# Graph layers and attention on one core: fourth sweep's sums and bias on TensorE with five tile pairs fetched ahead; fifth sweep's residual in one step

## The reference, cut to what matters

```
h = relu(adj @ (x @ W1) + b1)             # layer 1: 20 columns, second sweep
h = relu(adj @ (h @ W2) + b2)             # third sweep
h = relu(adj @ (h @ W3) + b3)             # fourth sweep: adj @ h has 20 columns, W3 makes 128
x = layernorm(x + relu(h + x))
fc = x @ W + b                            # layer 2, fifth sweep
x = layernorm(x + (adj * dinv[:,None] * dinv[None,:]) @ fc)
x = layernorm(x + adj @ x + gamma * attention(x))      # layer 3: sixth sweep, then attention
```

## Time and profile before

| | |
|---|---|
| median of 3 runs | 1342.76 us (1340.31 to 1343.25) |
| the profiled execution | 1341.3 us, span 1339.5 us |
| fourth sweep, from its first epilogue_1 to the end of its tiles | 454.3 to 530.8 us |
| fifth sweep | 530.8 to about 723 us |
| sixth sweep | to about 907 us |
| attention | the rest |
| granted TensorE clock | 0.994 of full, 1.00 in all the stretches below |

### The profile page before, as it was taken

How to read it: one execution, slowest core, us unless ns; L and a number is a source line. 1 busy time by engine, 2 the same in 40 slices (tenths; PEclk the granted TensorE clock), 3 DMA queues, 4 the chain that set the end, 5 groups by cost and what they waited for, 6 DMA issues and landing times.

```text
span 1339.5 us, 17278 instructions
## 1 busy us (share of the span) xinstructions
PE 1285.0 (96%) x5911; PEld 792.2 (59%) x5911; DVE 930.6 (69%) x1207; ACT 715.7 (53%) x880; POOL 267.5 (20%) x175
## 2 busy tenths in 40 slices
PE   8999999999999899999999999998899999999987
PEld 3544444433232233778787788886677767767764
DVE  6666665551010365999999989896888788788885
ACT  1111111011110123688787877776788788788795
POOL 0111110010000010011111100005234334354345
PEclk9999999998999999999999999999999999999999
DMA  9886665555999899899999999970000000000000
GB/s 367 314 316 251 251 219 204 173 188 181 382 333 400 309 352 407 307 353 374 351 371 359 376 356 361 382 291 0 1 0 1 1 1 1 1 18 14 1 1 32
DMA packets 81087, 288.01 MB, mean 215 GB/s; under 512 B 9466, under 2 KB 11130, under 8 KB 81018
## 3 DMA queue, kind: packets, MB, share of 16 engines
q1 hardware_dynamic: 78768, 286.30, 57.2%
q10 hardware_dynamic: 2250, 0.82, 0.2%
HBM read 284.98 MB, written 2.10 MB: 214 GB/s over the span
## 4 chain that ended last, share of the span: by engine, by line
PE 79%; DVE 8%; ACT 4%; issue 4%; DMA 3%; POOL 1%; POOLq 0%; ACTq 0%; DVEq 0%; SPq 0%
PE acc L1298 17%; PE acc L1536 7%; PE acc L1454 7%; PE acc L1388 7%; PE acc L1449 6%; PE acc L1450 6%; DMA raw<-in_adj_s 3%; DVE t_lo L1029 2%; PE rs L1306 2%; PE acc L1526 2%; PE acc L1527 2%; PE acc L1530 2%; PE e L1491 2%; PE e L1493 2%; PE rs L1491 2%
## 5 line engine op out<-in xcount | busy, mean ns | idle before, releaser
L1029 DVE TENSOR_TENSOR t_lo<-raw,t_hi 128x1024 fp32r<-128x1024 f32 x256 | 311.1, 1259 | 26.7 <-ACT t_hi L743 21.8
L743 ACT ACTIVATE t_hi<-raw 128x1024 fp32r<-128x1024 f32 x256 | 261.5, 1054 | 40.5 <-PE acc L1454 39.9
L1449 PE MATMUL acc<-t_hi,st_hi 128*128 128x512 f32 x512 | 201.9, 394 | 0.9 <-ACT t_hi L743 0.9
L1450 PE MATMUL acc<-t_hi,st_lo 128*128 128x512 f32 x512 | 199.5, 390 | 0.0
L613 POOL TENSOR_TENSOR ring_lo<-ring,p_hi 128x1024 fp32r<-128x1024 f32 x64 | 155.4, 2429 | 220.0 <-ACT p_hi L799 219.9
L1298 PE MATMUL acc<-raw,x 128*128 128x512 f32 x400 | 179.3, 597 | 0.0
L1454 PE MATMUL acc<-t_lo,st_hi 128*128 128x512 f32 x512 | 159.5, 393 | 5.8 <-DVE t_lo L1029 5.0
L1103 DVE TENSOR_TENSOR ring<-ring,e 128x1024 f32<-128x1024 f32 x128 | 154.0, 1212 | 0.1
L793 ACT ACTIVATE ring<-ring 128x1024 f32<-128x1024 f32 x128 | 134.2, 1054 | 25.0 <-DVE ring L1103 24.9
L1298 PEld LDWEIGHTS acc<-raw,x 128*128 128x128 f32 x400 | 73.7, 190 | 92.0 <-issue 92.0
L1536 PE MATMUL acc<-ring,x 128*128 128x512 f32 x256 | 120.2, 592 | 0.0
(11 more groups left out here) (220 smaller groups left out, 1878.8 us busy)
## 6 DMA issues: line engine op xcount, KB each, us to landing
raw<-in_adj_s SPq DMA_DIRECT2D x506, 512.0 KB, 5.7
kept_t<-in_adj_s SPq DMA_DIRECT2D x8, 512.0 KB, 6.6
x<-in_x SPq DMA_DIRECT2D x4, 512.0 KB, 10.3
kept_x<-in_adj_s SPq DMA_DIRECT2D x4, 512.0 KB, 6.4
kept_e<-in_adj_s SPq DMA_DIRECT2D x4, 512.0 KB, 7.7
kept_l<-in_adj_s SPq DMA_DIRECT2D x4, 512.0 KB, 6.5
kept_s<-in_adj_s SPq DMA_DIRECT2D x4, 512.0 KB, 6.7
kept_v<-in_adj_s SPq DMA_DIRECT2D x4, 512.0 KB, 6.9
```

Of the source, the lines that this page charges most:

```text
L743: nc.scalar.activation(t_hi[:, g % HL, :], raw[:, k, :], ACT.Copy).then_inc(hi_done, 1)
L1029: nc.vector.tensor_tensor(t_lo[:, k, :], raw[:, slot_no(s, c, g), :], t_hi[:, k, :].bitcast(F32), ALU.subtract).then_inc(lo_done, 1)
L1449: mm(a[:, :], block_of(st_h, b), hi[:, m], start=(g == 0 and j == 0), stop=False)
L1450: mm(a[:, :], block_of(st_l, b), hi[:, m], start=False, stop=False)
```

## The change

In the fourth sweep the copy from PSUM to `at` goes to ScalarE (`evacuate`), without adding `sums`. TensorE's epilogue_1 now adds three products for each of four blocks into e0: a constant 1/128 times the bias, `sums` times w3 (for c = 2 to 7), and `at` times w3. VectorE's bias step is gone. Five blocks (ten tiles) of the rows c = 2, 1 and 0 are no longer streamed through the ring: they are loaded into rooms whose tiles are used up, each as soon as the row named in ROOM_FREE is done.

In the fifth sweep the residual is one operation per block of 128 columns (times dinv, plus xb), four instead of two of 512 columns; residual_2 does nothing there. The remainder st5_lo goes from GpSimd to VectorE, after tile 12 of the rows from c = 2 on, and after tiles 3 and 13 of the sixth sweep's first row. 

```diff
-    "resid": (0, 3, 4), "b3": (3,), "lb": (3,), ...
+    "resid": (0, 3), "lb": (3,), ...
+AHEAD_3 = ((2, 4), (2, 5), (1, 3), (1, 4), (0, 2))
+ROOM_FREE = (0, 1, 2, 3, 3)
 def held(s, c, d):
-    return d in KEPT[c] and not (s == 0 and c == LATE)
+    return d in KEPT[c] and not (s == 0 and c == LATE) or s == 3 and (c, d) in AHEAD_3
...
+            def load_ahead(n):
+                c, d = AHEAD_3[n]
+                wait_row(sp, 3, ROOM_FREE[n])
+                for h in range(2):
+                    sp.dma_start(kept_tile(3, c, d, h), tile(c, 2 * d + h)).then_inc(ahead_in[n], 16)
...
                     sp.dma_start(raw[:, i.seq % RAW, :], tile(c, g)).then_inc(raw_in[i.seq % RAW], 16)
+                    while to_load and i.seq >= RAW and row_of[i.seq - RAW] > (3, ROOM_FREE[to_load[0]]):
+                        load_ahead(to_load.pop(0))
...
             def evacuate(s, c, par):
-                if s in NARROW:
+                if s in (1, 2):
                     return
...
                 elif s == 3:
+                    chunk = row(s, c)
+                    if stored(2, chunk):
+                        pe.wait_ge(sums_done, stored(2, chunk))
                     for b in range(CB):
-                        i = mm(block_of(e0, b), block_of(at, b), w3[:, :], start=True, stop=True)
+                        mm(block_of(e0, b), ones_d[:, 0:1].broadcast_to([P, P]), bias3[:, :], start=True, stop=False)
+                        if stored(2, chunk):
+                            mm(block_of(e0, b), block_of(sums[:, chunk, :], b), w3[:, :], start=False, stop=False)
+                        i = mm(block_of(e0, b), block_of(at, b), w3[:, :], start=False, stop=True)
...
                     elif s == 3:
-                        nc.vector.tensor_tensor(blocks(xs[:, :]), blocks(e0[:, :]), over_blocks(bias3[:, :]),
-                                                ALU.add).then_inc(S["b3"], 1)
-                        dve.wait_ge(S["b3"], done("b3", s, c))
                         dve.wait_ge(S["xb"], done("xb", s, c))
-                        nc.vector.scalar_tensor_tensor(out=xs[:, :], in0=xs[:, :], scalar=0.0, in1=xb[:, :],
+                        nc.vector.scalar_tensor_tensor(out=xs[:, :], in0=e0[:, :], scalar=0.0, in1=xb[:, :],
                                                        op0=ALU.max, op1=ALU.add).then_inc(S["t1"], 1)
                     else:
-                        nc.vector.tensor_tensor(blocks(xs[:, :]), blocks(e0[:, :]), spread(cols(dinv, c, CB)),
-                                                ALU.mult).then_inc(S["t1"], 1)
+                        dve.wait_ge(S["xb"], done("xb", s, c))
+                        scale = cols(dinv, c, CB)
+                        for b in range(CB):
+                            i = nc.vector.scalar_tensor_tensor(
+                                out=block_of(xs, b), in0=block_of(e0, b), scalar=scale[:, b:b + 1],
+                                in1=block_of(xb, b), op0=ALU.mult, op1=ALU.add)
+                        i.then_inc(S["t1"], 1)
...
+                    if s == S4 and g == 12 and not (isinstance(c, int) and c < 2):
+                        stationary5_lo(c - 2)
+                    if s == S5 and first(c) and g in (3, 13):
+                        stationary5_lo(NC - 2 if g == 3 else NC - 1)
```

More of the change, by code:

```diff
@@ L56, with summed @@
 }
+def summed(s):
+    return "t1" if s == 4 else "resid"
 def done(stage, s, r):
@@ L270, in build @@
         late_in = sem("late_in")
+        ahead_in = [sem(f"ahead_in{n}") for n in range(len(AHEAD_3))]
         S = {k: sem(f"s_{k}") for k in STAGES}
@@ L361, in wait_row, with kept_tile @@
                 eng.wait_ge(pe_acc, row_end(s, r))
-        def kept_tile(c, d, h):
+        def kept_tile(s, c, d, h):
+            if s == 3 and (c, d) in AHEAD_3:
+                n = AHEAD_3.index((c, d))
+                region, base = ((kept_v, 0), (kept_s, 0), (kept_l, 0), (kept_t, 0), (kept_t, 2))[n]
+                return region[:, base + h, :]
             n = 2 * KEPT[c].index(d) + h
@@ L370, in tile_of @@
         def tile_of(s, r, i):
-            return kept_tile(row(s, r), i.d, i.h) if i.kept else raw[:, i.seq % RAW, :]
+            return kept_tile(s, row(s, r), i.d, i.h) if i.kept else raw[:, i.seq % RAW, :]
         def wait_tile(eng, s, r, i):
             c = row(s, r)
+            if s == 3 and (c, i.d) in AHEAD_3:
+                eng.wait_ge(ahead_in[AHEAD_3.index((c, i.d))], 32)
+                return
             if not i.kept:
@@ L487, in load_kept @@
                     for h in range(2):
-                        sp.dma_start(kept_tile(c, d, h), tile(c, 2 * d + h)).then_inc(res_in, 16)
+                        sp.dma_start(kept_tile(0, c, d, h), tile(c, 2 * d + h)).then_inc(res_in, 16)
             def load_late():
@@ L493, in load_late @@
                     for h in range(2):
-                        sp.dma_start(kept_tile(LATE, d, h), tile(LATE, 2 * d + h)).then_inc(late_in, 16)
+                        sp.dma_start(kept_tile(0, LATE, d, h), tile(LATE, 2 * d + h)).then_inc(late_in, 16)
+            def load_ahead(n):
[3 more added lines that the diff above has]
+                    sp.dma_start(kept_tile(3, c, d, h), tile(c, 2 * d + h)).then_inc(ahead_in[n], 16)
+            row_of = {i.seq: (s, r) for (s, r), here in ITEMS.items() for i in here if not i.kept}
+            to_load = list(range(len(AHEAD_3)))
             def flat(s, r):
@@ L507, in flat @@
                         if s == 0 and c == 0:
-                            sp.dma_start(kept_tile(c, i.d, i.h), tile(c, g)).then_inc(row0_in[g], 16)
+                            sp.dma_start(kept_tile(s, c, i.d, i.h), tile(c, g)).then_inc(row0_in[g], 16)
                         continue
@@ L567, in step @@
                 ps, pc = before(s, c)
-                if s == S4 and not (isinstance(c, int) and c < 2):
-                    stationary5_lo(c - 2)
-                if s == S5 and first(c):
-                    stationary5_lo(NC - 2)
                 if has_before and ps in STAGES["xb"]:
@@ L583, in step @@
                     nc.gpsimd.tensor_copy(cols(x, row(ps, pc)), xn[:, :]).then_inc(S["xw"], 1)
-                if s == S5 and first(c):
-                    stationary5_lo(NC - 1)
             chunks(pool, step)
@@ L644, in evacuate @@
                     act.wait_ge(pe_acc, c + 1)
+                elif s == 3:
+                    wait_row(act, s, c)
                 else:
@@ L878, in stationary_lo, with stationary5_lo @@
                                         ALU.subtract).then_inc(st_lo_done, 1)
+            def stationary5_lo(d):
+                dve.wait_ge(st5_hi_done, d + 1)
+                nc.vector.tensor_tensor(cols(st5_lo, d), cols(x, d), cols(st5_hi, d).bitcast(F32),
+                                        ALU.subtract).then_inc(st5_lo_done, 1)
             def evacuate_narrow(s, r):
-                if s not in NARROW:
+                if s not in (1, 2):
                     return
```

16 lines of the change are left out of this document (6 added, 10 removed).

## The result

| | before | after |
|---|---|---|
| median | 1341.37 us (1338.35 to 1344.23, 16 runs) | 1344.20 us (1341.13 to 1347.43, 16 runs) |
| ratio | | 1.0024, 95% interval 1.0016 to 1.0032 |
| profiled execution, span | 1341.3, 1339.5 us | 1344.2, 1342.4 us |

The change makes the kernel slower, by 2.8 us between the medians and 3.2 us by the ratio (2.1 to 4.3 by its interval). I had forecast 2.2 us faster. The time lies inside the range, on the wrong side of zero. The sixteen executions of the changed kernel spread over 6.3 us, and the slow ones have the lower mean granted clock: 1341.13 us at 0.994, 1347.43 us at 0.989 (correlation -0.89).

What follows compares the result with a forecast made beforehand. Fourth sweep: early rows bound by the `at` chain, late rows by loads; fifth: TensorE waiting on VectorE. Terms 3.6 - 1.2 - 4.5 - 0.1 = -2.2 us gave 1339.1, by the median 1340.6 us; range 1333 to 1347.

Steps and rivals of the forecast that it cites:

- Term A: Fourth sweep: eight more products in the chain cost more than VectorE saves; +3.6 us, bounds -5 and +7.
- Term B: Fifth sweep's first row: VectorE does less ahead of the norm TensorE waits for; -1.2 us, between -2 and 0.
- Term C: Fifth sweep's six rows from c = 2: the t_lo wait goes, 22.45 us per row; -4.5 us, bounds -5.4 and 0.
- Term D: Sixth sweep's first row: two remainders come onto VectorE, two GpSimd subtracts go; -0.1 us, between -1 and +1.
- Twelve products at 0.272 us, 3.27: Fourth sweep's epilogue_1: twelve products at the old four's 0.272 us each take 3.27 us.
- The loads drop out: Fourth sweep's late rows: with ten tiles moved early, the sweep becomes bound by the chain and TensorE, not loads.
- All of them stand behind TensorE's wait for `at`, although only four need it: Fourth sweep's epilogue_1: all twelve products, 3.27 us, follow the wait; eight of them, 2.18 us, do not need `at`.
- 1.45 us of waiting before epilogue_3 in two rows: Fourth sweep's rows 6 and 7: TensorE reaches epilogue_3 before the norm, waiting 1.45 us that only loads hid.
- TensorE's own work in the row with two pairs of epilogues, 13.6: Fourth sweep's row 5: 14 tiles and two pairs of epilogues take TensorE 13.6 us.
- The load queue does not stall: Fourth sweep's new loads: each stands behind a ring tile whose own wait already implies the freed room.
- Rival 3: Fourth sweep pays more, Term A near +7 by waits before epilogue_3 and late loads: +1.2, 1344 us; chance 0.10.
- rival 2: VectorE fills up in the fifth sweep, Term C near 0, kernel slower: +2.3, 1345.5 us; chance 0.18.

Runs made afterwards that it cites:

- e1: Kernel before with only the fifth sweep's edits (residual in one step per block, st5_lo on VectorE): 1337.61 us, ratio to before 0.9980.
- e12: e8 with the last two tile pairs fetched one and two rows later (ROOM_FREE changed): 1337.63 us, ratio to the kernel before 0.9976.
- e14: Changed kernel with the last two tile pairs fetched later, when rows 4 and 5 have ended: 1342.97 us, ratio to the kernel before 1.0013.
- e5b: Changed kernel with the products of bias and sums issued before TensorE's wait for `at`: 1340.46 us, ratio to the kernel before 0.9997.
- e2: Kernel before with only the ten tiles fetched ahead; sums and bias stay on VectorE: 1345.99 us, ratio to before 1.0042.
- e7: Kernel before with only st5_lo moved to VectorE: 1338.25 us, ratio to before 0.9978.
- e9: Changed kernel with ScalarE copying `at` of the fourth sweep's second row before normalising the first row: 1341.68 us, ratio to the kernel before 1.0004.
- e8: e1 with the ten tiles fetched ahead, sums and bias still on VectorE: 1342.67 us, ratio to the kernel before 1.0015.
- e4: Changed kernel without the added products in epilogue_1, bias and sums left out of the result: 1336.99 us, ratio to the kernel before 0.9971.

## Why the prediction was wrong

**Term A is the step that failed: +3.6 forecast (its own starts give 3.7), +7.5 measured** in the profiled executions. The ratios can't part A from B: from e1 to the changed kernel both come in, and they measure +5.9 for the two together, where +2.4 was forecast and the profiles have +6.0. C and D together are e1: -2.7 by its ratio (-3.8 in the changed kernel's profile), where -4.6 was forecast. With A and B as forecast, the measured -2.7 would still have left the kernel a little faster; with A and B as measured, even the forecast -4.6 would have left it slower.

Row by row of the fourth sweep (a row is the time from one epilogue_1 to the next):

| row | forecast us | measured us | what the trace has there |
|---|---|---|---|
| 1 | 9.4 | 8.9 | products 2.95 for 3.27 |
| 2 | 9.4 | 10.5 | clock at 0.50 for 3 us behind the wait of 4.13 |
| 3 | 10.0 | 10.1 | |
| 4 | 10.8 | 12.3 | wait of 1.25 for a streamed tile |
| 5 | 13.6 | 14.6 | TensorE busy all the time, two pairs of epilogues |
| 6 | 14.0 | 14.6 | wait of 1.93, not 1.45, before epilogue_3 |
| 7 | 12.0 | 13.0 | wait of 1.92, not 1.45, before epilogue_3 |
| spread over 4 to 7 | 1.0 | | |
| sum | 80.2 | 84.0 | |

The parts of the term, in its own words:

- *Twelve products at 0.272 us, 3.27*: measured 2.95, so this part was even too dear.
- *"The loads drop out", "no TensorE waits for loads"*: wrong. I compared each row's bytes with its time and left out the order in the queue, where four tiles for much later rows went ahead of those of the next row. e12 shows the mechanism: 5.0 us where products are not in the way. In the changed kernel itself it shows as 1.25 us of waiting, and e14's 1.5 us are not clear of the noise.
- *"All of them stand behind TensorE's wait for `at`, although only four need it"*: said, and priced by length alone. The wait itself grew from 3.34 to 4.13 us behind ScalarE's norm, and then the clock fell: 1.6 us more for that epilogue_1, a term that the sum put at nothing. e5b, with the order changed, took 3.6 us away. The mean granted clock of all executions went up with it, from 0.991 to 0.993 (0.993 before the change).
- *1.45 us of waiting before epilogue_3 in two rows*: right in kind, 1.93 and 1.92 measured. In e2, where VectorE still has the bias step, it is 3.00 and 2.65.
- *TensorE's own work in the row with two pairs of epilogues, 13.6*: 14.6, and the engine didn't wait. The parts named for it add up to 13.3 with one 0.65 for the changes between kinds of product; two of them would be 14.0.
- *"The load queue does not stall"*: wrong in fact (2.9 us), without effect as far as seen: e12 has the same 2.9 us and no wait for a streamed tile behind it.

Rival 3 (A near +7, by waits before epilogue_3 and late loads) is nearest to what happened; I gave it 0.10. Its two causes were in my text, and I counted one at 1.45 us and the other at nothing. That its 1344 meets the measured 1344.20 is luck: it was reckoned as +1.2 us on a median of three runs, 1342.76, and the change was about +3 on 1341.37.

**Term B**, -1.2: -1.5 in the profiles. **Term D**, -0.1: -0.7. **Term C**, -4.5: measured -3.1 (six rows, 23.2 to 22.7). The mechanism was right: without the subtract two t_lo take 2.36 us again (they took 3.15), the copy beside two others costs 0.41 (0.40 forecast), and four residual operations 1.04 (1.03 forecast). The size was off because I took TensorE's floor from another row, 22.3 at c = 1. TensorE was itself busy 22.51 in the rows meant, and now it is busy 22.60 of 22.70. This also decides against rival 2: VectorE, with 21.8 to 22.0 us, did not fill up.

The Trainium skill ("SBUF — State Buffer", "Who interferes with whom") was weighed for term C: its full exclusion would have freed up to 1.3 us of VectorE per row. The subtract's removal (e7) took two t_lo from 3.15 to 2.36 us with the copy moved away as well, so the trace agrees in direction and puts the sum for both GpSimd instructions at 0.79 us. The 2.9 us of GpSimd's work that I set against it were not all beside these two t_lo: the subtract began at 631.42, the two t_lo at 632.19, so 0.53 us of the subtract and the whole copy (1.61 us) were.

What stays open: how e9's 2.7 us divide, since its one profile shows 1.7 and loses them to the clock; how much of each kernel's time is the clock (kernels that lose have a lower mean, 0.989 in e2 and e8 against 0.993 before, but e4 and e12 have 0.990 and are fast); and whether fetching ahead, mended, gains over e1 (0.9965 against 0.9980, on different chips and with overlapping intervals).

## What to carry to other kernels

A transfer that is moved earlier in a queue goes ahead of something. List, for every queue, which load it now precedes and when that one is needed; bytes per row against time per row does not show it. When a resource stops being the limit, look for steps whose place was chosen for the old pace (here epilogue_3, eight tiles behind epilogue_1), and move them with it. Work that doesn't need the awaited operand belongs before the wait: over the sweep, the products without `at` cost 3.6 us less ahead of it than behind it.
